# Attention and routed experts on one core: the experts' first layer in half-width products

## The reference

```python
x = x + attention(layernorm(x), qkv_w, qkv_b, proj_w, proj_b)      # 16 heads of 16, causal, with rope
h = layernorm(x)
aff = h @ centroids.T                        # (4096, 8)
e = argmax(aff, axis=1)                      # one expert for each token
alpha = sigmoid(aff[token, e])
t = layernorm(h) * ln_g[e] + ln_b[e]
t = relu(t @ w1[e].T + b1[e])                # 256 -> 1024
y = h + t @ w2[e].T + b2[e]                  # 1024 -> 256
x = x + alpha * y + (1 - alpha) * h
```

## Time and profile before

| | us |
|---|---|
| median of 2 runs | 948.38 (948.35 to 948.42) |
| the profiled execution's own time | 948.4 |
| its span from first to last instruction | 946.3 |
| TensorE busy with products in the span | 870.7 |
| TensorE busy with weight loads | 517.7 |
| VectorE, ScalarE, GpSimd busy | 603.1, 534.9, 315.7 |

### The profile page before, as it was taken

The page is one execution under the profiler, slowest core; times in us unless marked ns, Lnnn a source line. Parts: engine busy times, 40 slices in busy tenths (PEclk is TensorE's granted clock), DMA queues, the critical chain, the costliest instruction groups (busy, mean ns, idle before and its releaser), DMA issues. The chain is left out here.

```text
span 946.3 us, 20352 instructions
## 1 busy us (share of the span) xinstructions
PE 870.7 (92%) x6606; PEld 517.7 (55%) x6655; DVE 603.1 (64%) x1111; ACT 534.9 (57%) x1338; POOL 315.7 (33%) x471
## 2 busy tenths in 40 slices
PE   7999869999999999999999989924999999999996
PEld 4555413333333333333333326613999999999996
DVE  5888999888888888888888306861333333323332
ACT  4667437777777877877777874661322232232221
POOL 9988644333332232232333321461111111111111
PEclk9999979999999999999999999966999999999998
DMA  7588442422521112222213207345666566656660
GB/s 263 168 255 248 143 130 96 157 69 69 169 69 47 48 49 65 69 68 69 69 56 105 90 1 240 122 165 204 211 192 210 194 197 193 219 185 199 199 212 6
DMA packets 55139, 130.68 MB, mean 138 GB/s; under 512 B 9753, under 2 KB 30874, under 8 KB 48794
## 3 DMA queue, kind: packets, MB, share of 16 engines
q1 hardware_dynamic: 49482, 108.19, 36.7%
q0 software_dynamic: 5584, 21.54, 6.0%
HBM read 101.21 MB, written 28.48 MB: 137 GB/s over the span
## 5 line engine op out<-in xcount | busy, mean ns | idle before, releaser
L802 ACT ACTIVATE arena<-ps_pair 128x512 f32<-128x512 f32 (+3 forms) x768 | 328.9, 494 | 102.2 <-PE ps_pair L1134 94.7
L891 DVE TENSOR_REDUCE B_block_max<-ps_item 128x8 f32<-128x1024 f32 x288 | 340.5, 1220 | 40.9 <-PE ps_item L1041 37.8
L1134 PE MATMUL ps_pair<-q_stack,k_stack 99*128 99x512 bf16 (+5 forms) x720 | 182.3, 330 | 12.4 <-ACT arena L802 6.8
L717 POOL TENSOR_SCALAR_AFFINE_SELECT arena<-arena 128x256 f32<-128x256 f32 x256 | 103.9, 406 | 202.6 <-ACT arena L802 200.2
L1150 PE MATMUL ps_pair<-arena,B_v_quad 128*32 128x512 f32 (+3 forms) x1536 | 163.6, 498 | 1.0 <-ACT B_oacc L816 0.7
L1134 PEld LDWEIGHTS ps_pair<-q_stack,k_stack 99*128 99x128 bf16 (+1 forms) x768 | 54.0, 97 | 187.4 <-ACT arena L802 170.2
L1686 PEld LDWEIGHTS D_ps_h<-D_xT,arena 128*128 128x128 f32 x1248 | 147.8, 195 | 4.6 <-ACT D_xT L1624 2.7
L1686 PE MATMUL D_ps_h<-D_xT,arena 128*128 128x128 f32 x1248 | 148.3, 278 | 2.1 <-ACT D_xT L1624 2.1
L1705 PE MATMUL D_ps_y<-arena,D_hr 128*128 x624 | 141.0, 379 | 0.0
L1615 ACT ACTIVATE D_hr<-D_ps_h,ffn_columns 128x128 f32<-128x128 f32 x156 | 44.5, 368 | 165.4 <-PE D_ps_h L1686 165.4
L1598 POOL DMA_INDIRECT out<-D_res,D_ids x39 | 38.4, 984 | 259.5 <-issue 200.9
(11 more groups left out here) (163 smaller groups left out, 730.6 us busy)
## 6 DMA issues: line engine op xcount, KB each, us to landing
arena<-in_w_exp SPq DMA_DIRECT2D x39, 1024.0 KB
qk_parts<-arena SPq DMA_DIRECT2D x32, 384.0 KB, 3.5
q_stack<-qk_parts SPq DMA_DIRECT2D x96, 128.0 KB, 3.0
rows<-payload SPq DMA_DIRECT2D x39, 257.0 KB, 2.7
arena<-in_x SPq DMA_DIRECT2D x16, 512.0 KB, 6.2
k_stack<-qk_parts SPq DMA_DIRECT2D x64, 128.0 KB, 3.0
arena<-in_w_exp POOLq DMA_DIRECT2D x8, 1024.0 KB, 6.8
arena<-in_x_feat SPq DMA_DIRECT2D x8, 512.0 KB, 5.8
```

Source lines behind the costliest of these rows:

```text
L717: pool.affine_select(out=block_p, in_=block_p, compare_op=ALU.is_ge, fill=0.0, base=0, pattern=[[0, 2], [1, P]], channel_multiplier=-1).th ...
L802: act.activation(pr[s % PR][:, h, 0:QW - off], ps_s[(QH * s + j) % R][:, 0:QW - off], ACT.Exp, scale=scale).then_inc(s_e, 1)
L891: dve.tensor_reduce(bmx[:, g:QH:GH, first:first + 3 * gap + 1:gap], src[:, :, :].rearrange("p c (b n) -> p c b n", n=P), AX.X, ALU.max).th ...
L1134: pe.matmul(ps_s[(QH * s + j) % R][:, 0:QW - off], ks[rows, r, half, bass.ds(g * SEQ + kb * P, P)], qs[rows, r, half, bass.ds(g * SEQ + c ...
```

## The change

Each product of the first layer is issued as two: the same 128x128 weight tile is multiplied with the slot's first 64 tokens and, behind both halves `c` of the input, again with its last 64 (`HALF` = 64). The two write the left and the right half of the same columns of the same bank. The sum over `c` is inside. The waits and signals are where they were.

```diff
                         for f in range(FC):
                             if f % HC == 0:
                                 wait(pe, s_r[f // HC], S, HC, 0)
-                            for c in range(DC):
-                                at = c * FF + f * P
-                                mm = pe.matmul(ps_h[f // HC][:, f % HC, :], w1b[:, r, at:at + P], xT[:, r, c, :],
-                                               start=(c == 0), stop=(c == DC - 1))
+                            for lo in (0, HALF):
+                                for c in range(DC):
+                                    at = c * FF + f * P
+                                    mm = pe.matmul(ps_h[f // HC][:, f % HC, lo:lo + HALF], w1b[:, r, at:at + P],
+                                                   xT[:, r, c, lo:lo + HALF], start=(c == 0), stop=(c == DC - 1))
                             if f % HC == HC - 1:
                                 mm.then_inc(s_m1[f // HC], 1)
```

## The result

The changed kernel takes 1101.0 us (1100.4 to 1101.6) against 948.4 us: 1.161 times as long, with a 95% interval from 1.156 to 1.166. That is 13 us above the forecast of 1088 us and 1 us above its range, which ended at 1100 us.

The account below looks back on a forecast made before the run. TensorE's stream in the expert stage was taken as the bound, with weight loads setting the first layer's pace. 948.4 us plus 139.3 us from term one, all other terms 0, gave 1088 us (+14.7%), range 1078 to 1100 us.

Parts of the forecast that it names:

- The bound: Expert stage: TensorE is busy throughout at full clock, so every nanosecond its stream gains is paid at the end.
- the count: First layer: the doubled calls make 2496 loads and 2496 products, 64 of each in a slot.
- term one: First layer, all slots: 32 more load-and-product pairs at 111.6 ns, 3.57 us a slot, +139.3 us over 39 slots.
- The load's rule: First layer's weight loads: columns over 1.2 GHz, 106.7 ns for 128, would make the whole 1075 us; trace rows preferred.
- The rule of streaming: First layer, first rival: streaming sets the pace, 55.8 ns for 64 columns, time stays 948.4 us; 4% together with omitted reloads.
- Terms three to five: Expert stage: other engines, transfers and longer loop code each add 0; refetched code could cost up to 22 us.
- term two: Slot 0's start at half clock: new pairs mostly follow the clock's rise; taken as 0, 3 us kept for the range.
- My second rival: First layer in the slots: short products lose the full clock, +250 us to 1338 us, or some 1480 us; 7%.
- the code: Expert loop, third rival: longer body does not stay on chip, 8 rounds fetch 1 to 2.7 us, 1096 to 1110 us; 8%.

Follow-up runs that it names:

- e5_left_half: Changed kernel with slots 0 and 1 unsplit and the right 64 tokens of the first layer left out from slot 2 on: 942.8 us, 0.999 of the kernel before.
- e1_wide_start: Changed kernel with slots 0 and 1 unsplit (128-column products) and slots 2 to 38 split: 1079.9 us, 1.136 times the kernel before.
- e2_split_start: Kernel before the change with only slots 0 and 1 split, slots 2 to 38 unsplit: 968.9 us, 1.021 times the kernel before.
- e3_split_warm: Changed kernel with 8 products of 256 columns into an unused bank ahead of slot 0: 1092.4 us, 1.151 times the kernel before.

## Why the prediction was wrong, and where it was right

The bound was right: from slot 2 on TensorE's stream is the path, without a gap, and all of its growth is paid. So was the count, 2496 loads and products, and term one, the price that decides the result: 111.6 ns forecast, from the first layer's own distance and the eight products with 8 columns, 110.8 measured. Over slots 2 to 37 the forecast was 128.5 us and the trace shows 127.0. e5_left_half shows the mechanism alone: with half the columns and as many loads the time does not move. The load's rule of the Trainium skill ("TensorE: Matmul & The Clock Gate", LDWEIGHTS), 106.7 ns, is 4% too low for these float32 tiles. The rule of streaming (the Trainium skill, "TensorE: Matmul & The Clock Gate", Back-to-back issue gap), by which nothing would have changed, does not set the pace here. I had it too strong in the prediction: the page gives that formula for single products without their loads, and says itself that it comes out too low for short ones.

Terms three to five were right at 0: nothing waits in the split slots, the DMA share fell to 0.43, and in the loop's rounds behind the first no instruction packet moves. The packets of the first round cost nothing that the chain shows; the slots there have the same 10.77 us. The body of 656 loads and products stays on the chip. The Trainium skill's 2048 instructions for TensorE ("Runtime: NRT & Kernel Launch", Instruction fetch mechanics) would have it so, and the trace agrees up to that length.

The step that failed is term two, the start. I wrote that the 32 new pairs of slot 0 "come behind the old ones and mostly behind that rise", and kept 3 us for the range. That took the rise as an event at a time, which the change could only miss by the new pairs. The runs showed that it hangs on what TensorE does there, which the change alters. The engine was as busy as before by its column and had half as many columns per load to stream, and the clock stood at 0.50 through both first slots. The excess over the 3.5 us that the change costs in any other slot is 4.3 us in slot 0 and 7.8 us in slot 1, 12.1 us against the 0 that I took and the 3 us that I kept. e1_wide_start and e2_split_start show it from both sides, and e3_split_warm takes it away with a clock that is up. My second rival had the mechanism, but I asked only whether a risen clock would fall in mid-stage, where the rows of the attention stage spoke against it, and not whether one that was down would come up. The rows that I had for the start were those of 128-column products. The Trainium skill ("TensorE: Matmul & The Clock Gate", HAM oscillation) warns of idle gaps in TensorE's work as what costs the clock. To heed that would not have been enough: in slot 0 TensorE worked from 654.57 us for 13.9 us without a gap, and the clock stayed at 0.50.

The 2.3 us by which the stage begins later in the profiled execution need no cause in the change, since that time scatters by more. The first transposes come at 645.4 us in the trace of e5_left_half and at 656.2 us in that of e1_wide_start, and nothing ahead of them differs between the kernels. Without these 2.3 us the number would have come to lie inside the range, but by luck: its upper end was there for the code, which cost nothing. The 12.1 us of term two do not hang on it.

## What to carry to other kernels

Before making a product narrower, find what sets the distance between starts: an instruction with very few columns elsewhere in the trace gives the load's own pace. Once streaming takes less than that, a product made still narrower costs the full price of its load. If a float32 product must be cut, cut the stationary side into column halves: here that cost 0.3 us a slot (one run), and cutting the tokens 3.5 us. And look at the clock's rise at the head of a stage as something that the stage's own products have to bring about: the same change cost 3.5 us a slot once the clock was up, and 7.8 and 11.4 us in the two slots before.

## What was not expected of the hardware

Short products show two sides. With 64 columns behind each load of a whole tile the clock, once up, stayed at 2.4 GHz to the end of the stage, with a second layer of wide products in each slot, and in e3_split_warm through two slots with none between them. Down, it did not rise in 29 us of such products (e2_split_start, and the changed kernel). With 32 columns it fell in each slot, after 3.4 us in the first one. And float32 products on column halves of the array overlapped: a pair of load and product every 57.7 ns with 128 columns streamed in each, against 108 ns one after another.
